# Layer 1 of a two-layer conditioned transformer block: two ScalarE steps done by GpSimd

## What is computed

```
xn = layer_norm(x) * w + b
q, k = xn @ q_w + q_b, xn @ k_w + k_b
att = softmax(q k^T + (1 - mask) * -1e6)
v  = (xn @ v_w + v_b) * mask
y  = att @ v
h  = layer_norm(y) * (1 + scale) + shift      # scale, shift from the condition
out = x + silu(h) @ out_w + out_b
```

## Time and profile before

| | |
|---|---|
| median of 3 runs | 1352.57 us (1350.74 to 1353.4) |
| the profiled execution | 1350.56 us |
| its span, first to last instruction | 1348.8 us |
| PE busy | 1306.4 us (97%) |
| DVE busy | 1029.0 us (76%) |
| ACT busy | 994.5 us (74%) |
| POOL busy | 346.2 us (26%) |

### The profile page before, as it was taken

How to read it: one execution, slowest core, us unless ns; L and a number is a source line. 1 busy time by engine, 2 the same in 40 slices (tenths; PEclk the granted TensorE clock), 3 DMA queues, 4 the chain that set the end, 5 groups by cost and what they waited for, 6 DMA issues and landing times.

```text
span 1348.8 us, 25657 instructions
## 1 busy us (share of the span) xinstructions
PE 1306.4 (97%) x9592; PEld 1044.4 (77%) x9592; DVE 1029.0 (76%) x2121; ACT 994.5 (74%) x2259; POOL 346.2 (26%) x367
## 2 busy tenths in 40 slices
PE   8999999999999999899999999999999999999998
PEld 5778888888888877568788788787787787786666
DVE  5888878788797977666876876976876876977656
ACT  5354544454545467788998998998998998998884
POOL 0323234342324361100410410400400500500302
PEclk9999999999999999899899899999899899999879
DMA  9111111212112346674464464465464455554512
GB/s 340 46 40 63 40 63 42 100 36 68 63 40 87 102 157 205 203 205 134 143 187 147 147 188 145 156 174 152 148 173 150 160 163 158 165 151 127 160 38 87
DMA packets 83998, 173.79 MB, mean 129 GB/s; under 512 B 7305, under 2 KB 8329, under 8 KB 83873
## 3 DMA queue, kind: packets, MB, share of 16 engines
q1 hardware_dynamic: 83872, 172.14, 41.1%
HBM read 104.45 MB, written 67.14 MB: 127 GB/s over the span
## 4 chain that ended last, share of the span: by engine, by line
PE 69%; ACT 12%; DVE 10%; issue 2%; SPq 2%; DMA 2%; POOL 2%; DVEq 0%; POOLq 0%; ACTq 0%
PE ps L527 14%; PE ps L529 13%; PE ps L528 13%; PE ps L712 9%; ACT ps L894 7%; PE ps L694 6%; PE ps L686 6%; PE ps L522 6%; ACT Pb L904 3%; DVE cT L1171 2%; DVE st L1005 1%; PE ps L636 1%; PE ps L615 1%; POOL yb L1344 1%; DMA mask_scratch<-vhl 1%
## 5 line engine op out<-in xcount | busy, mean ns | idle before, releaser
L1171 DVE TENSOR_REDUCE cT<-ps 128x1 f32<-128x512 f32 x512 | 321.7, 682 | 65.7 <-PE ps L686 65.0
L894 ACT ACTIVATE ps<-ps,cT 128x512 f32<-128x512 f32 x512 | 352.5, 770 | 21.9 <-DVE cT L1171 21.8
L904 ACT ACTIVATE Pb<-ps 128x512 f32<-128x512 f32 x512 | 271.1, 668 | 34.0 <-PE ps L694 33.3
L686 PE MATMUL ps<-Ks,Qs 98*128 98x512 f32 x512 | 198.3, 450 | 16.3 <-ACT ps L894 14.6
L894 ACT ACTIVATION_READ_ACCUMULATOR ps<-ps,cT 128x1 f32 x512 | 162.2, 317 | 0.0
L694 PE MATMUL ps<-Qs,Ks 100*128 100x512 f32 x512 | 159.0, 407 | 3.2 <-DVE sg_q L1162 1.3
L686 PEld LDWEIGHTS ps<-Ks,Qs 98*128 98x128 f32 x512 | 100.3, 198 | 77.8 <-ACT ps L894 48.8
L1344 POOL TENSOR_TENSOR yb<-yb,cU 128x512 f32<-128x512 f32 x14 | 20.5, 1486 | 426.2 <-DVE cU L1217 426.2
L694 PEld LDWEIGHTS ps<-Qs,Ks 100*128 100x128 f32 x512 | 95.9, 189 | 38.1 <-ACT Pb L904 11.0
L527 PE MATMUL ps<-xTh,Wh_k 128*128 128x512 f32 x256 | 106.7, 417 | 7.6 <-DVE xTl L1022 4.5
L1268 POOL TENSOR_TENSOR rs<-ve,mhalf 128x4 f32<-128x4 f32 x32 | 33.0, 1031 | 291.6 <-DVE ve L990 221.0
(11 more groups left out here) (169 smaller groups left out, 2924.4 us busy)
## 6 DMA issues: line engine op xcount, KB each, us to landing
Qs<-stack_scratch SPq DMA_DIRECT2D x32, 768.0 KB
Ks<-stack_scratch SPq DMA_DIRECT2D x32, 768.0 KB
stack_scratch<-sg_q SPq DMA_DIRECT2D x32, 512.0 KB, 2.7
stack_scratch<-sg_k SPq DMA_DIRECT2D x32, 512.0 KB, 2.6
wr<-in_x SPq DMA_DIRECT2D x32, 256.0 KB, 4.6
x_scratch<-wr SPq DMA_DIRECT2D x32, 256.0 KB, 2.0
stack_scratch<-sg_q SPq DMA_DIRECT2D x32, 256.0 KB, 2.9
stack_scratch<-sg_k SPq DMA_DIRECT2D x32, 256.0 KB, 2.9
```

The lines of the kernel that those rows point to most:

```text
L686: e.matmul(bank[:], Qs[par][0:RX, j, t * 128:(t + 1) * 128], Ks[par][0:RX, j, :], start=True, stop=True).then_inc(s["S"], 1)
L894: e.activation(bank[:], bank[:], ACT.Exp, bias=nx[:, n % 2, j, t, 0:1], accum_out=dn[:, b % 2, t, 4 * g + j:4 * g + j + 1]).then_inc(s["S_ ...
L904: e.activation(Pb[m][:, j, :], ps[bank_of["a", n, m, j]][:], ACT.Exp).then_inc(s["P"], 1)
L1171: e.tensor_reduce(nx[:, n % 2, j, t, 0:1], ps[bank_of["S", n, j, t]][:], AX.X, ALU.max, negate=True).then_inc(s["S_max"], 1)
```

## The change

ACT's two steps go to POOL for the items of layer 1, with exceptions. The mask on the values: for items 9 to 15 DVE's bias add now writes to the SBUF buffer and not to PSUM, and POOL multiplies there in place; the bank is free when DVE is done (`v_add`). Item 8 stays as it was. The rounding to `sTh`: for items 8 to 14 POOL does it, just ahead of its `sTl`; item 15 stays as it was.

```diff
@@ done @@
             if k == "v":
-                return s["v_lo" if key[1] < 8 else "v_hi"], 4 * key[1] + key[2] + 1
+                return s["v_lo" if key[1] < 8 else "v_hi" if key[1] == 8 else "v_add"], 4 * key[1] + key[2] + 1
@@ scalar @@
             def v(i, x, t):
-                if i == 5:
+                if i == 5 and x <= 8:
...
                         if t == 0:
                             e.wait_ge(s["tx"], 4 * x + 4)
-                        if x == 8 and t == 0:
                             e.wait_ge(s["l_mk"], 32)
...
                     if c == 0 and x:
                         e.wait_ge(s["o_mm"], 4 * x)
+                    if not in_bank(x):
+                        return
                     e.wait_ge(s["y_s"], 4 * x + c + 1)
                     ch, _, at = half(x, c)
                     e.copy(tok(x, sTh[:, ch, at]), s_tile(x, c)).then_inc(s["s_hi"], 1)
@@ vector @@
                     e.wait_ge(s["v_mm"], n)
-                    e.tensor_tensor(ps[bank_of["v", x, t]][:], ps[bank_of["v", x, t]][:], bvB[:], ALU.add).then_inc(s["v_add"], 1)
+                    if x > 8 and t == 0:
+                        e.wait_ge(s["tx"], 4 * x + 4)
+                    dst = ps[bank_of["v", x, t]][:] if x <= 8 else xbuf(x)[:, t, :]
+                    e.tensor_tensor(dst, ps[bank_of["v", x, t]][:], bvB[:], ALU.add).then_inc(s["v_add"], 1)
@@ gpsimd @@
+            def v(i, x, t):
+                if i == 5 and x > 8:
+                    e.wait_ge(s["v_add"], 4 * x + t + 1)
+                    row = xbuf(x)[:, t, :]
+                    e.tensor_scalar(row, row, mk[:, x % 8, t:t + 1], None, ALU.mult).then_inc(s["v_hi"], 1)
...
                     if x < 15:
                         if c == 0:
                             e.wait_ge(s["o_mm"], 4 * x)
+                        e.wait_ge(s["y_s"], 4 * x + c + 1)
+                        e.tensor_scalar(t4(sTh[:, c, :]), yb[:, :, c * 128:(c + 1) * 128], 1.0, None, ALU.mult).then_inc(s["s_hi"], 1)
                         e.wait_ge(s["s_hi"], 4 * x + c + 1)
                         e.tensor_tensor(t4(sTl[:, c, :]), yb[:, :, c * 128:(c + 1) * 128],
                                         t4(sTh[:, c, :].bitcast(F32)), ALU.subtract).then_inc(s["s_lo"], 1)
...
-            parts = {"nx": nx_, "ny": ny, "q": q, "qn": qn, "o": o, "ty": ty, "ones": ones, "tlx": tlx}
+            parts = {"nx": nx_, "ny": ny, "v": v, "q": q, "qn": qn, "o": o, "ty": ty, "ones": ones, "tlx": tlx}
```

## The result

The changed kernel takes 1358.44 us (median of 9 runs, 1355.89 to 1360.53) against 1353.40 us for the kernel before, measured beside it (9 runs, 1350.74 to 1355.30). The ratio is 1.0040, with a 95% interval of 1.0029 to 1.0051: slower by 5 us, where a gain of 3 had been forecast. The time lies outside the range. In kind it is rival C, to which the prediction gave 1 in 10.

A forecast was written before the change was run, and what follows sets the result against it. PE bounds the kernel, starved only in an item's first part, where it waits for ACT's exponentials. Gains of 2.45 (masks) and 0.5 (item 14) make 3.0 us: median 1352.57 to 1349.6 us, range 1345.5 to 1354.0.

The forecast's parts named there:

- rival C: POOL's rounding is late, so PE waits for `sTl` in items 8 to 13: 11.6 us lost, 1361.2 us; 1 in 10.
- the price of a rounding on POOL: Length of one rounding on POOL, not in the trace: taken as 0.77 us, between bounds 0.77 and 1.52.
- h: One rounding on POOL plus the 0.15 us until `sTl` starts: 0.92 us.
- The prediction's own formula: End of the fourth `sTl` on POOL: 760.7 + 4h + 6 x 1.25 + 1.29 = 769.49 + 4h, giving 773.2.
- 1.1 of slack: Time between the fourth `sTl`'s end and PE's need of it, 1.1 us where there was 0.84: no loss.
- The threshold of 1.19: The h above which the fourth `sTl` misses PE's 774.24: (774.24 - 769.49) / 4 = 1.19 us.
- The upper bound named: Longest length allowed for POOL's rounding: 1.52 us, from L1344 with two inputs and a broadcast.
- The masks: At the first value tile of items 9 to 15, PE's wait on ACT's mask goes: 7 x 0.35 = 2.45 us saved.
- Item 14: POOL rounds the fourth chunk early, so PE's 0.84 us wait goes; 0.5 us counted as gain.
- The roundings' slack on ACT: ACT's 0.51 us roundings in the second part are covered by PE's full queue: no gain from removing them.
- DVE charged nothing: New POOL work does not slow DVE: L1142 took 0.69 us with POOL busy or idle, so zero cost.
- The rule quoted beside it: Skill's limit on the GPSIMD and DVE port conflict: only DVE instructions with two SBUF inputs or a two-port mode.

The follow-up runs named there:

- e1: Changed kernel with the four masks and four roundings of an item each in a different POOL instruction form; 1353.44 us (one run).
- e8: Changed kernel with only POOL's rounding in the two-operation form (multiply, add 0.0), masks left one-operation; 1348.54 us, ratio 0.9975 to the kernel before.
- e6: Kernel before with only the roundings moved to POOL, in two-operation form, masks on ACT; 1351.65 us, ratio 1.0003 to the kernel before.
- e4: Changed kernel with an item's four bias adds on POOL moved behind its fourth `sTl`; 1354.05 us, ratio 0.9999 to the kernel before.
- e7: As e4, plus a POOL wait ahead of the bias adds until DVE's two small TENSOR_SCALARs are done; 1355.74 us, ratio 1.0026 to the kernel before.

## Why the prediction was wrong

**The step that failed** is the price of a rounding on POOL: "it has one input and a constant, so I take 0.77", from L1290. It measured 1.50 (e1 shows why: L1290 has two operations, the rounding one). With the 0.08 to the start of `sTl`, h is 1.58 and not 0.92. The prediction's own formula then gives 769.49 + 4 x 1.58 = 775.8 for the fourth `sTl`, against PE's 774.24: 1.6 us late, where 1.1 of slack had been computed. The formula itself was right: from first rounding to the end of the fourth `sTl` the chain took 15.12 us (761.86 to 776.98), and it gives 15.11. The threshold of 1.19 agrees with the runs, which do not test it closely: at 0.62 + 0.08 there is no wait, at 1.58 there is one in each item.

The upper bound named was 1.52, from L1344, and the truth lay at that bound. What misled was the choice between the ends by the count of inputs. The TENSOR_TENSORs of that shape (1.1 to 1.5) were set aside for it; the short rows (L1281 and L1290) were both of one form, two operations, and the trace of before had no TENSOR_SCALAR with one operation on POOL of that size.

**Rival C's size** was too large: 11.6 us lost, where e8 against the kernel after shows 8.8, some 1.5 in each of six items and not 1.9. Most of it is h: the formula with 1.58 in place of 1.67 gives 1.57 an item and 9.4 in all, which the 8.8 can't be told from. In the profile the six waits add up to less still, 7.7, and they differ from item to item. The reason is seen in two stretches of the kernel after, `pv` ahead of the two places above:

```profile
759.50:764.40 4.90, 4.90 (x130) 4.51 (x129) 4.74 (x9) 2.96 (x6) 2.46 (x2) 0.73 0.50 119
860.71:864.34 3.63, 3.63 (x129) 3.57 (x128) 3.49 (x8) 2.30 (x6) 1.15 (x1) 0.94 0.17 39
```

The same matmuls took 1.27 us longer in the first, at a granted clock of 0.73 instead of 0.94. PE's lateness at `sTl` there was 0.54 and not 1.73. POOL's first rounding started 21.65 us after the item's first L1356 in both (740.21 to 761.86, 841.54 to 863.19), so what PE loses to its clock comes off the wait: 1.27 + 0.54 is about 1.73 again. The six items bear it out. From the item's first L1356 to the matmul that waited, five of them take 36.80 to 36.84 us and one 37.18, though `pv` took from 3.7 to 5.0 us in them. A chain on another engine sets the length of this stretch, and PE's own slowness is hidden beside it.

**The masks** were right in mechanism: 0.35 us at the place named, in the profile to the hundredth, no L807 waits left, DVE's write to SBUF as long as that to PSUM (0.689 against 0.697), and POOL's side free. It is free even at twice the length forecast.

**Item 14**: the wait of 0.84 is gone, as computed. How much of it is kept can't be told from 0.5, or from nothing.

**The roundings' slack on ACT** was worth nothing, as said (e6). This was the main argument, that it matters where ACT loses work and not how much, and it held.

**DVE charged nothing** was wrong in a small part. The row looked at was L1142, with one input in SBUF. The rule quoted beside it names two kinds of DVE instruction that do contend, and L990 and L991, TENSOR_SCALARs from SBUF to SBUF, can be of the second kind; I didn't look for them. The 1.3 us against 0.16 of e4, and their going in e7, show that these two are held. What it costs in the changed kernel stays open; the two longest holds there fall into PE's wait for `sTl`.

**Of the chances**: the threshold of 1.19 stands for a rounding of 1.04 (less the 0.15), well inside the bounds of 0.77 and 1.52. An even spread over the prediction's own bounds would have given 6 in 10 to a rounding above it, so the 1 in 10 for C was too little.

## What to carry to other kernels

When a chain on an idle engine gets a new link, its price times its count is set against the slack at the chain's end; where the threshold (the price at which the slack is gone) lies between the two bounds of an unmeasured price, the chance is split there, and not given to the nearer-looking row. Price an instruction by one of the same form (the number of operations included), not only of the same shape and inputs. And write a scaling or a rounding on POOL with two operations, the second one adding 0.0, or as a copy, and time it.

## What the hardware showed that was not expected

A TENSOR_SCALAR of POOL with one operation (a multiply) takes 1.50 to 1.56 us for 128x512 elements, with two operations (multiply, add) 0.62 to 0.77, a copy 0.62. The Trainium skill (GPSIMD Engine Reference, Engine selection) calls one-input work there "roughly line-rate". That fits the copy and the two-operation form (DVE's 128x512 took 0.69), and not the one-operation form. Why it differs no run here shows.

DVE's TENSOR_SCALARs of 128x4 elements were held by POOL until one of its 1.3 us instructions ended: 1.34 us instead of 0.16. The smaller the instruction, the less its busy time makes one look for this.
